# Moving the first attention's mask addition from VectorE to GpSimd and rearranging the order of a slot on every engine

## The reference, cut to what matters

```
def attention(q, k, v, mask):
    scores = jnp.einsum('bhqd,bhkd->bhqk', q, k) / jnp.sqrt(jnp.float32(HD))
    scores = scores * mask - 10000.0 * (1.0 - mask)
    probs = jax.nn.softmax(scores, axis=-1)
    return jnp.einsum('bhqk,bhkd->bhqd', probs, v)
ln_out = layernorm(hidden_states, ln1_s, ln1_b)
q, k, v = jnp.split(ln_out @ w_qkv + b_qkv, 3, axis=-1)
x = hidden_states + merge_heads(attention(q, k, v, ltor_mask)) @ w_ao + b_ao
q = layernorm(x, ln2_s, ln2_b) @ w_q + b_q
k, v = jnp.split(encoder_states @ w_kv + b_kv, 2, axis=-1)
x = x + merge_heads(attention(q, k, v, cross_mask)) @ w_co + b_co
return x + gelu(layernorm(x, ln3_s, ln3_b) @ w1 + b1) @ w2 + b2
```

## Time and profile before

| what | value |
| --- | --- |
| three runs | 961.91, 963.16 and 963.85 us, median 963.16 |
| the profiled execution | 962.38 us, of which the span from the first to the last instruction is 960.6 |
| TensorE, matmuls | 918.6 us busy (96% of the span) |
| TensorE, weight loads | 767.8 us (80%) |
| VectorE | 591.4 us (62%) |
| ScalarE | 462.9 us (48%) |
| GpSimd | 413.3 us (43%) |
| mean granted clock of TensorE | 0.996 of full speed |

### The profile page before, as it was taken

One profiled execution on the slowest core, in us unless ns is written; L12 is line 12 of the kernel. 1 busy time (PEld: TensorE's weight loads), 2 busy tenths in 40 slices (PEclk: granted clock), 3 DMA queues, 4 the chain that ended last, 5 costly groups with the idle time before them and its releaser, 6 DMA issues.

```text
span 960.6 us, 23348 instructions
## 1 busy us (share of the span) xinstructions
PE 918.6 (96%) x9345; PEld 767.8 (80%) x9345; DVE 591.4 (62%) x974; ACT 462.9 (48%) x1026; POOL 413.3 (43%) x572
## 2 busy tenths in 40 slices
PE   6999989988999999999999999999998999899998
PEld 4777767976778889888887888888887888678775
DVE  5899986776654343544356443344436757998883
ACT  3677775237743433333435333333333344566565
POOL 2143345965346443423256443343323952343231
PEclk9999999999999999999999999999999999999999
DMA  9100000410011101112101110111100100000000
GB/s 295 47 23 2 2 1 2 140 56 1 2 56 51 53 26 44 53 51 56 56 8 56 51 56 25 55 40 56 51 24 18 56 1 1 2 1 7 12 7 23
DMA packets 24177, 37.64 MB, mean 39 GB/s; under 512 B 4432, under 2 KB 16528, under 8 KB 23824
## 3 DMA queue, kind: packets, MB, share of 16 engines
q1 hardware_dynamic: 24080, 36.23, 12.2%
HBM read 35.17 MB, written 1.05 MB: 38 GB/s over the span
## 4 chain that ended last, share of the span: by engine, by line
PE 70%; DVE 14%; ACT 6%; POOL 5%; issue 5%; DMA 0%; SPq 0%; DVEq 0%; ACTq 0%; POOLq 0%
PE ps L1299 18%; PE ps L790 13%; PE ps L1316 10%; PE ps L1957 6%; PE ps L1334 4%; PE ps L890 3%; PE ps L1360 3%; PE ps L1344 2%; DVE sb L2485 2%; DVE sb L656 1%; DVE sb L650 1%; PE ps L2035 1%; PE ps L421 1%; PE ps L270 1%; PE ps L2121 1%
## 5 line engine op out<-in xcount | busy, mean ns | idle before, releaser
L837 POOL TENSOR_TENSOR sb<-sb 128x256 fp32r<-128x256 f32 (+1 forms) x128 | 102.0, 797 | 255.3 <-DMA sb<-in_heads_a 135.3
L1299 PE MATMUL ps<-sb 128*128 128x512 f32 x768 | 188.4, 395 | 1.0 <-issue 1.0
L1299 PEld LDWEIGHTS ps<-sb 128*128 128x128 f32 x768 | 139.5, 188 | 33.7 <-issue 6.1
L790 PE MATMUL ps<-sb 128*128 128x256 f32 x1152 | 148.8, 286 | 0.2 <-DVE sb L936 0.2
L790 PEld LDWEIGHTS ps<-sb 128*128 128x128 f32 x1152 | 141.5, 191 | 2.6 <-issue 0.6
L839 POOL TENSOR_TENSOR sb<-sb 128x256 fp32r<-128x256 f32 (+1 forms) x128 | 118.4, 925 | 10.0
L1511 DVE TENSOR_REDUCE sb<-ps 128x8 f32<-128x520 f32 x32 | 22.4, 700 | 126.3 <-PE ps L1334 126.3
L1316 PE MATMUL ps<-sb 128*128 128x256 f32 x768 | 99.1, 285 | 0.4 <-DVE sb L1499 0.4
L1316 PEld LDWEIGHTS ps<-sb 128*128 128x128 f32 x768 | 95.0, 191 | 3.0 <-issue 0.9
L1434 ACT ACTIVATE sb<-ps,sb 128x512 f32<-128x512 f32 x64 | 43.8, 685 | 107.4 <-PE ps L1299 107.4
L1531 DVE SCALAR_TENSOR_TENSOR sb<-ps,sb 128x512 fp32r<-128x512 f32 x64 | 45.1, 746 | 72.1 <-ACT sb L1467 72.1
(11 more groups left out here) (221 smaller groups left out, 1674.5 us busy)
## 6 DMA issues: line engine op xcount, KB each, us to landing
sb<-in_heads_a SPq DMA_DIRECT2D x32, 386.0 KB, 3.1
sb<-in_heads_c SPq DMA_DIRECT2D x16, 256.0 KB, 3.8
sb<-in_heads_b SPq DMA_DIRECT2D x32, 128.0 KB, 3.2
sb<-in_mlp_a SPq DMA_DIRECT2D x16, 128.5 KB, 2.0
sb<-in_mlp_b SPq DMA_DIRECT2D x16, 128.0 KB, 2.1
sb<-in_w_r SPq DMA_DIRECT2D x1, 2048.0 KB, 7.6
sb<-in_encT SPq DMA_DIRECT2D x1, 1024.0 KB, 6.4
sb<-in_ctx SPq DMA_DIRECT2D x1, 1024.0 KB, 8.3
```

Source lines behind the costliest of these rows:

```text
L790: last = pe.matmul(m.acc(t), lhsT[x], rhs[w], start=opens and n == 0, stop=False, skip_group_check=True)
L837: pool.tensor_tensor(high, src, one, ALU.mult).then_inc(*G.did(name + "_high", u))
L1299: last = pe.matmul(m.ps[u][:, c, :], m.w_parts[u][w][:, (KD * q + k) * P:(KD * q + k + 1) * P], rows[x][:, k, c * 512:(c + 1) * 512], star ...
```

## The change

`masked` moves to GpSimd for the first 15 items; the last item's stays on VectorE (`masked_last`). `top` waits for GpSimd's counter in place of VectorE's own. The loops of all four engines get another order:

- TensorE: `keys` directly behind `scores`, `query` behind `turn_probs`; `values` of this slot's item (before: of the item one slot earlier, at the head of the slot), and `turn` of the next item, between `turn_context` and `out`.
- ScalarE: `exp` at the head of the slot after the one in which `shifted` runs; `normed` and `rows` for the item of the next slot.
- VectorE: `add` one slot later, at the head of the slot; `stats` and `variance` two items ahead; `context` ahead of `top` and `shifted`, and all three behind `keys`.
- GpSimd: `rstd` two items ahead, `masked` ahead of it, `row_split` and `row_bias` behind `bias`.

No transfer is added, removed or moved in SyncE's queue.

```diff
@@ attn0_tensor
+    turn(0)
+    keep_warm(pe, m.z2, ..., 3)
+    pe.wait_ge(m.s_wqkv, 32)
     for slot in range(SLOTS):
         scores(slot - 1)
+        keys(slot)
+        warm(slot == SLOTS - 2, 3)
         turn_probs(slot - 2)
-        values(slot - 1)
-        turn(slot)
-        if slot == 0:
-            keep_warm(pe, m.z2, ..., 3)
-            pe.wait_ge(m.s_wqkv, 32)
-        warm(slot == SLOTS - 2, 3)
-        context(slot - 2)
+        query(slot)
         if slot == SLOTS - 1:
             fc2(pe, ph, m, 0, 0, 0)
             fc1(pe, ph, m, 4, 0, 0, 1)
         turn_rows(slot - 3)
-        keys(slot)
+        context(slot - 2)
+        values(slot)
         if slot in (SLOTS - 3, SLOTS - 2):
...
             fc1(pe, ph, m, 4, u, 0, 0)
         turn_context(slot - 2)
-        query(slot)
+        turn(slot + 1)
         warm(slot in (SLOTS - 3, SLOTS - 2), 3)
         out(slot - 2)
@@ attn0_scalar
     normed(0)
+    rows(0)
     for slot in range(SLOTS):
+        exp(slot - 2)
+        if slot == SLOTS - 2:
+            act.activation(m.bv[0][:, :], m.col("eps"), ACT.Gelu_apprx_tanh)
+        if slot:
+            normed(slot + 1)
+        keys(slot)
+        row_normed(slot - 3)
         turn_probs(slot - 2)
-        row_normed(slot - 3)
-        values(slot - 1)
-        rows(slot)
+        query(slot)
         if slot == SLOTS - 2:
             gelu_rows(act, ph, m, ACT.Gelu_apprx_tanh, 0, 0, 0)
         mlp_rows(slot - 3)
-        keys(slot)
         context(slot - 2)
...
-        query(slot)
-        exp(slot - 1)
-        if slot == SLOTS - 3:
-            act.activation(m.bv[0][:, :], m.col("eps"), ACT.Gelu_apprx_tanh)
-        normed(slot + 1)
+        values(slot)
+        if slot == 0:
+            normed(1)
+        rows(slot + 1)
@@ attn0_vector
-    @of_item
-    def masked(i):
...
+    def masked_last():
...
     def top(i):
-        vec.wait_ge(*m.own_vec.at("masked", i))
+        vec.wait_ge(*(m.own_vec if i == LAST_ITEM else m.own_pool).at("masked", i))
...
     for slot in range(SLOTS):
+        add(slot - 3)
         row_stats(slot - 3)
         row_variance(slot - 3)
         multiplied(slot - 1)
...
-        masked(slot - 1)
-        top(slot - 1)
-        context(slot - 2)
-        shifted(slot - 1)
+        if slot == LAST_ITEM + 1:
+            masked_last()
         keys(slot)
         if slot == 0:
             vec.wait_ge(m.s_x[1], 16)
-        stats(slot + 1)
-        variance(slot + 1)
+            stats(1)
+            variance(1)
+        stats(slot + 2)
+        variance(slot + 2)
+        context(slot - 2)
+        top(slot - 1)
+        shifted(slot - 1)
         if slot == SLOTS - 2:
             mlp_split(vec, ph, m, 0, 0, 0)
-        add(slot - 2)
@@ attn0_gpsimd
+    @of_item
+    def masked(i):
+        if i == LAST_ITEM:
+            return
...
+        pool.wait_ge(*done["mul"].at(i))
+        pool.tensor_tensor(probs, probs, bc(masks, 1, [P, NH0, S]), ALU.add).then_inc(*m.own_pool.did("masked", i))
...
+    rstd(0)
+    rstd(1)
     for slot in range(SLOTS + 1):
-        if slot == 0:
-            rstd(0)
         if slot == SLOTS:
             split_fc1(pool, ph, m, 0, 1, streams=(1,))
+        row_rstd(slot - 3)
+        masked(slot - 1)
+        rstd(slot + 2)
+        bias(slot)
         row_split(slot - 4)
         if slot == SLOTS - 1:
             split_fc1(pool, ph, m, 0, 1, streams=(0,))
-        row_rstd(slot - 3)
-        bias(slot)
         row_bias(slot - 4)
-        rstd(slot + 1)
```

More of the change, by code:

```diff
@@ L259 @@
 SLOTS = len(ITEMS) + 3
+LAST_ITEM = len(ITEMS) - 1
 FIRST_WEIGHTS = 4
@@ L440, in attn0_tensor @@
     pe.wait_ge(m.s_const, 16 * m.n_const)
+    turn(0)
+    keep_warm(pe, m.z2, m.vdiag[0][:, :, :, :, :].rearrange("p b n o e -> p (b n o e)")[:, 0:512], 3)
+    pe.wait_ge(m.s_wqkv, 32)
     for slot in range(SLOTS):
         scores(slot - 1)
+        keys(slot)
+        warm(slot == SLOTS - 2, 3)
         turn_probs(slot - 2)
-        values(slot - 1)
-        turn(slot)
-        if slot == 0:
-            keep_warm(pe, m.z2, m.vdiag[0][:, :, :, :, :].rearrange("p b n o e -> p (b n o e)")[:, 0:512], 3)
-            pe.wait_ge(m.s_wqkv, 32)
-        warm(slot == SLOTS - 2, 3)
-        context(slot - 2)
+        query(slot)
         if slot == SLOTS - 1:
@@ L454, in attn0_tensor @@
         turn_rows(slot - 3)
-        keys(slot)
+        context(slot - 2)
+        values(slot)
         if slot in (SLOTS - 3, SLOTS - 2):
             u = slot - (SLOTS - 3)
-            pe.wait_ge(*(done["qT"], done["pT1"])[u].at(len(ITEMS) - 1))
+            pe.wait_ge(*(done["qT"], done["pT1"])[u].at(LAST_ITEM))
             fc1(pe, ph, m, 4, u, 0, 0)
         turn_context(slot - 2)
-        query(slot)
+        turn(slot + 1)
         warm(slot in (SLOTS - 3, SLOTS - 2), 3)
@@ L651, in multiplied @@
                           ALU.mult).then_inc(*done["mul"].did(i))
-    @of_item
-    def masked(i):
-        vec.wait_ge(*done["mul"].at(i))
-        vec.tensor_tensor(probs(i), probs(i), mask(m.mask_add, i), ALU.add).then_inc(*m.own_vec.did("masked", i))
+    def masked_last():
+        vec.wait_ge(*done["mul"].at(LAST_ITEM))
+        vec.tensor_tensor(probs(LAST_ITEM), probs(LAST_ITEM), mask(m.mask_add, LAST_ITEM), ALU.add)\
+            .then_inc(*m.own_vec.did("masked", LAST_ITEM))
     @of_item
     def top(i):
-        vec.wait_ge(*m.own_vec.at("masked", i))
+        vec.wait_ge(*(m.own_vec if i == LAST_ITEM else m.own_pool).at("masked", i))
         vec.tensor_reduce(m.mx[i % 2][:, 0:NH0], probs(i), AX, ALU.max).then_inc(*m.own_vec.did("max", i))
@@ L740, in row_rstd @@
         norm_scales(pool, m, t % 2, 1, ("attn0_rows_pow", t), row["rstd"].did(t))
+    @of_item
+    def masked(i):
+        if i == LAST_ITEM:
+            return
+        kind, t = ITEMS[i]
+        if i in (0, ITEMS.index(("cross", 0))):
+            pool.wait_ge(m.s_masks, ATTN0.index(kind) + 1)
+        masks = m.mask_add[kind] if kind == "self" else m.mask_add[kind][:, t, :]
+        probs = m.p0[i % 2][:, :].rearrange("p (n t) -> p n t", t=S)
+        pool.wait_ge(*done["mul"].at(i))
+        pool.tensor_tensor(probs, probs, bc(masks, 1, [P, NH0, S]), ALU.add).then_inc(*m.own_pool.did("masked", i))
     @of_item
```

## The result

The change made the kernel slower by half a percent: 966.44 us as a median of six runs (963.55 to 967.80) against 962.11 of six runs of the kernel before (960.37 to 963.85), a ratio of 1.0051 with an interval of 1.0037 to 1.0065. The forecast was 960.5, in a range of 957.0 to 964.0. The profiled execution after took 963.55 us, the fastest of its six, with a span of 961.8, where before had 962.38 and 960.6.

A forecast was written before the change was run, and what follows sets the result against it. VectorE was taken to bound slots with rows, TensorE and its waits the others. 3.5 us gained in the middle less 0.9 at the end gave 2.6, so 963.16 became 960.5 us, range 957.0 to 964.0.

The forecast's parts named there:

- The slot: Slots 3 to 15: TensorE's work plus its wait before `out` gives 8.24 us, 8.52 with rows; 3.5 us gained.
- the stand-still in front of `out`: In each slot TensorE waits 0.53 us for ScalarE's copies, since `query` no longer fills that gap.
- The addition: On GpSimd an estimated 2.35 us per item, hidden with 0.9 us to spare before `top` starts.
- ScalarE answers late: Rival: `turn_context` to `out` takes 1.40 us each time, 13 slots lose 3.0 us, median 963.5; chance 0.22.
- the addition lands on the path: Rival: GpSimd's addition takes 4.92 us, slots last 8.96 and 9.75 us, time 972.4; chance 0.10.
- The MLP behind it is shifted as a whole: After the stage: the MLP and later blocks move by the summed gain of 2.6 us.
- The masks of slot 4: Masks staying in slot 4 cost nothing, with VectorE at 6.4 and GpSimd at 5.6 of 8.24 us.
- the one such operation left: VectorE's subtraction, reading two SBUF tensors, alone meets GpSimd's hold: put at 0, at most 0.4 us per slot.
- The start: Slots 0 to 2: clock pauses change, between 1.7 us gained and 1.7 lost; taken as 0.
- The end: Slots 16 and 17: nothing covers the exponential, 0 to 2.1 us lost; taken as 0.9.

The follow-up runs named there:

- e2: The kernel before, with the first stream's weight split put behind `row_rstd` in GpSimd's last slot: 965.57 us, ratio 1.0058 to the kernel before.
- e1: The kernel after, with the first stream's weight split put back ahead of `row_rstd` in GpSimd's last slot: 963.28 us, ratio 1.0036 to the kernel before.
- f3: e1 with the second stream's weight split also ahead of the last row scale: 960.94 us, ratio 0.9996 to the kernel before.
- e4: e1 with the mask's addition back on VectorE for all items, ahead of `keys`: 962.70 us, ratio 1.0023 to the kernel before.
- f2: The kernel after, with VectorE's two operations on the second attention's masks moved from slot 4 to slot 1: 964.28 us, ratio 1.0048 to the kernel before.
- e7: The kernel before unaltered, traced in another execution: 959.42 us.
- e3: The kernel after unaltered, run and traced again: median 965.99 us, ratio 1.0053 to the kernel before.
- e6: e1 unaltered, traced for a third profile: 960.16 us.
- e5: e1 unaltered, traced for a second profile: 963.95 us.
- f1: The kernel after, with three dummy matmuls in TensorE's pauses at the start: 966.48 us, ratio 1.0067 to the kernel before.
- f4: The kernel after, with both weight splits ahead, the second masks in slot 1 and three dummy matmuls at the start: 957.30 us, ratio 0.9970 to the kernel before.

## Why the prediction was wrong, step by step

- **The slot: right.** 8.24 and 8.52 us forecast, 8.05 and 8.32 measured; the stand-still in front of `out` 0.53 forecast, 0.50 measured; 3.5 us gained forecast, 4.07 measured although slot 4 took 2.0 too much. VectorE idles 1.40 us in the slot shown (0.63 and 0.77) instead of two.
- **The addition: right.** 2.35 estimated, 2.36 measured; 0.9 us to spare, 0.86 measured. "ScalarE answers late" and "the addition lands on the path" did not occur; neither explains the loss.
- **"The MLP behind it is shifted as a whole": the step that failed first.** The walk followed GpSimd's queue through a middle slot and never through slot 18, where the diff moves the weight split behind `row_rstd`. That turned a gain of 3.50 us at the last `out` into a loss of 1.20 at `fc2`: 4.70 us, of which the wait is 3.67 and the slow `fc1` behind it 1.38 (2.93 - 1.55); the 0.40 that TensorE waited before `turn_rows` in the kernel before is no longer there. e2 shows the mechanism in the old order, e1 and f3 its removal.
- **The masks of slot 4, "I cost them at nothing": wrong by 2.0 us.** The text priced the hold between GpSimd and VectorE for the subtraction alone, "the one such operation left". L699 reads one tensor and took 2.47 us instead of 0.43 all the same (e4, f2).
- **The start, "I take 0", bounds of 1.7 either way: too narrow below.** The 0.78 us gained in the profiled pair (30.40 against 31.18) is the fall in the old one's trace: without a fall the old order has 30.37 (e7). With a fall the new order lost 2.0 to 2.8 against 31.18 (33.2 to 34.0). This is the likely reason why the other five runs of the kernel after lie 2.6 to 4.3 us above its profiled one; none of the five was traced, but e3, the same kernel at 967.46, shows the fall.
- **The end, 0.9 of 0 to 2.1:** from the scores to the `out` of the last item 16.02 us (138.39 to 154.41) against 14.67 before, so 1.35 lost. That lies within its bounds, but for another reason than the one given. TensorE's wait for the exponential there is 0.43 us, and 0.37 before; what is new are waits for ScalarE's `row_normed`, 1.9 us in two slots where the kernel before has none.

```profile
141.65 0.44 PE L430 MATMUL ps<-sb 128*128 128x128 f32 x2 [0.65 <-ACT sb L230]
150.16 0.44 PE L430 MATMUL ps<-sb 128*128 128x128 f32 x2 [1.28 <-ACT sb L230]
```

For the profiled pair the terms close: 0.78 gained at the start, 4.07 in the middle, 1.35 lost at the end, 4.70 in slot 18, in sum 1.20 us lost. The difference of the medians is 4.33; the remaining 3.1 us belong to executions that were not all traced. The profiled pair had its fall at the start in the old order only. Against e7, which had none, the kernel after gained nothing at the start, its `fc2` came 2.04 us late (163.64 against 161.60), and its span is 4.2 us longer.

## What to carry to other kernels

When an order written out by hand is changed for the middle of a pipeline, walk each queue through its last slots too: an instruction that some other block needs, there the weight split, must not stand behind one that waits for the last item. When GpSimd takes over a long operation, look for every VectorE instruction between SBUF tensors that runs beside it, also those that occur once. And the engine's price ratio says little by itself: the same addition of 2.4 us gained 4 us with other work in VectorE's queue between producer and consumer, and cost 40 without it and with the row scale behind it in GpSimd's queue.

## What the runs showed of the hardware that was not expected

A tensor_scalar of 128x512 with one SBUF input lasted 2.47 us instead of 0.43 beside GpSimd's addition of 128x1024 (e4, f2 against the kernel after). The same program ran its first 22 us at full clock in one execution and at 0.54 from 15 to 22 us in another (e6, e5). And in f1's trace, where the pauses at the start were filled, the clock fell behind the next one, in slot 4. The ratio, 1.0053 in e3, was 1.0067 with f1 alone and 1.0048 with f2 alone; both splits ahead brought it to 0.9996 (f3), and all three repairs to 0.9970 (f4).
